# State-space steps on one Trainium2 core: the sums over states as quarter-array products

## What is computed

```python
delta = softplus(dt @ W_dt.T + b_dt)          # 512 channels
dA = exp(delta[..., None] * A)                # 16 states for each channel
dBx = delta[..., None] * Bm[:, :, None, :] * xc[..., None]
h = dA_t * h + dBx_t                          # scan over the 512 positions
y = einsum('bles,bls->ble', hs, Cm) + xc * Dp # sum over the 16 states, and the skip
y = y * silu(z)
out = einsum('ble,de->bld', y, W_out)
```

## Time and profile before

| what | value |
|---|---|
| median of 3 runs | 824.77 us (823.97 to 1462.39) |
| the profiled execution, its own time | 824.44 us |
| its span in the profile | 822.6 us |
| mean granted TensorE clock | 0.969 |

### The profile page before, as it was taken

One profiled execution on the slowest core, in us unless ns is written; L12 is line 12 of the kernel. 1 busy time (PEld: TensorE's weight loads), 2 busy tenths in 40 slices (PEclk: granted clock), 3 DMA queues, 4 the chain that ended last, 5 costly groups with the idle time before them and its releaser, 6 DMA issues.

```text
span 822.6 us, 10341 instructions
## 1 busy us (share of the span) xinstructions
PE 737.9 (90%) x3787; PEld 523.0 (64%) x3823; DVE 548.4 (67%) x962; ACT 395.8 (48%) x575; POOL 240.8 (29%) x182
## 2 busy tenths in 40 slices
PE   3899999996788899999999998996889998788997
PEld 3587565652435466667877886884547787435786
DVE  4444589999969999964456556358754655943543
ACT  3354596666465687732232343351375532274321
POOL 0000058775438587850896000001000000000000
PEclk9899999999999899999999998999799999999999
DMA  8300022222102222217001000033000142000000
GB/s 278 129 2 0 1 66 78 76 71 67 55 28 64 65 76 62 82 39 225 13 1 22 0 1 1 14 102 103 16 2 1 56 115 62 2 28 1 1 1 25
DMA packets 30591, 41.75 MB, mean 51 GB/s; under 512 B 3753, under 2 KB 19955, under 8 KB 30515
## 3 DMA queue, kind: packets, MB, share of 16 engines
q1 hardware_dynamic: 29290, 40.91, 16.7%
q10 hardware_dynamic: 1252, 0.19, 0.2%
HBM read 36.73 MB, written 4.26 MB: 50 GB/s over the span
## 4 chain that ended last, share of the span: by engine, by line
PE 64%; DVE 15%; issue 11%; ACT 4%; DMA 4%; SPq 2%; DVEq 0%
PE PS L489 34%; PE PS L859 7%; DVE PS L1947 4%; PE PS L589 3%; PE PS L1050 3%; PE PS L1067 3%; DVE shared L1955 2%; PE PS L634 2%; ACT shared L1543 2%; PE PS L843 1%; DVE route L2000 1%; PE PS L447 1%; DMA scratch_k<-shared 1%; DMA shared<-in_L_ffn_W_dram 1%; SPq L2212 1%
## 5 line engine op out<-in xcount | busy, mean ns | idle before, releaser
L2258 POOL TENSOR_TENSOR shared<-shared,route 128x1024 f32<-128x1024 f32 x64 | 151.4, 2368 | 78.7 <-DVE shared L1955 73.5
L489 PE MATMUL PS<-xnT,weights_r 128*128 128x256 f32 (+1 forms) x732 | 156.3, 361 | 0.5 <-issue 0.3
L489 PE MATMUL PS<-xnT,work_r 128*128 128x512 f32 (+1 forms) x596 | 150.4, 401 | 0.2 <-DVE gated L1723 0.2
L1955 DVE TENSOR_TENSOR_SCAN shared<-shared,PS 128x512 f32<-128x512 f32 x128 | 148.7, 1203 | 1.4 <-ACT shared L1487 1.4
L489 PEld LDWEIGHTS PS<-xnT,weights_r 128*128 128x128 f32 x732 | 115.4, 190 | 34.0 <-issue 20.1
L489 PEld LDWEIGHTS PS<-xnT,work_r 128*128 128x128 f32 (+1 forms) x596 | 110.7, 191 | 24.7 <-DVE gated L1723 0.4
L859 PE MATMUL PS<-shared,cf 128*128 128x512 f32 x256 | 124.7, 610 | 0.0
L1487 ACT ACTIVATE shared<-shared,cols 128x512 f32<-128x512 f32 x128 | 85.0, 715 | 29.6 <-DVE shared L1955 29.2
L1723 DVE TENSOR_TENSOR gated<-gated,PS 128x512 f32<-128x512 f32 (+1 forms) x52 | 35.6, 685 | 91.2 <-ACT gated L1235 91.1
L489 PE MATMUL PS<-weights_r,work_r 128*128 128x256 f32 (+1 forms) x624 | 92.5, 298 | 3.6 <-DVE work_r L1730 2.6
L489 PEld LDWEIGHTS PS<-weights_r,work_r 128*128 128x128 f32 (+1 forms) x624 | 82.1, 193 | 6.4 <-DVE work_r L1730 3.2
(11 more groups left out here) (218 smaller groups left out, 1027.2 us busy)
## 6 DMA issues: line engine op xcount, KB each, us to landing
route<-scratch_c SPq DMA_DIRECT2D x64, 256.0 KB, 3.2
shared<-in_L_ffn_W_dram SPq DMA_DIRECT2D x3, 1024.0 KB, 9.2
scratch_k<-shared SPq DMA_DIRECT2D x12, 128.0 KB
scratch_q<-shared SPq DMA_DIRECT2D x12, 128.0 KB
shared<-scratch_k SPq DMA_DIRECT2D x8, 192.0 KB
shared<-scratch_q SPq DMA_DIRECT2D x8, 192.0 KB
mamba_w<-in_L_ffn_w_dram SPq DMA_DIRECT2D x2, 704.0 KB, 5.5
beside<-in_L_ffn_w_dram SPq DMA_DIRECT2D x2, 704.0 KB, 7.6
```

The lines of the kernel that those rows point to most:

```text
L489: last = nc.tensor.matmul(o, lhs[l], rhs[r], start=(start and i == 0), stop=(stop and i == 2))
L1955: v.tensor_tensor_scan(hst[:, (t % 2 * 2 + j) * T:(t % 2 * 2 + j + 1) * T], decay[t % D_SLOTS][:, j * T:(j + 1) * T], products[:, j * T:(j ...
L2258: nc.gpsimd.tensor_tensor(hc[:, u * 2 * T:(u + 1) * 2 * T].rearrange("p (c t) -> p c t", c=2), hst[:, (t % 2) * 2 * T:(t % 2 + 1) * 2 * T] ...
```

## The change

`add_state` forms each of its two sums in two products of 64 rows by 64 columns, on four different quarters of the array. Rows 0 to 63 of chunk 0 go to partitions 0 to 63 of bank 4, rows 0 to 63 of chunk 1 to partitions 64 to 127 of bank 5; rows 64 to 127 of chunk 0 to partitions 64 to 127 of bank 4, and those of chunk 1 to partitions 0 to 63 of bank 5. So the two halves of chunk 1's sum lie crosswise in bank 5, and `add_skip` reads them with two instructions of 64 partitions in place of one of 128.

```diff
@@ -51,6 +51,7 @@
 SUM_BANKS = (4, 5)
+HALF_ROWS = (slice(0, 64), slice(64, 128))
@@ -855,10 +856,12 @@
                 def add_state(t, of=b):
                     pe.wait_ge(s["hc"], HEAD + of * STEPS + t + 1)
-                    for j in range(2):
-                        last = nc.tensor.matmul(bank(SUM_BANKS[j]), ident[:, :],
-                                                hc[:, (t % H_SLOTS * 2 + j) * T:(t % H_SLOTS * 2 + j + 1) * T],
-                                                start=False, stop=(t % DS == DS - 1))
+                    for r in HALF_ROWS:
+                        for j in range(2):
+                            o = HALF_ROWS[r.start // 64 ^ j]
+                            last = nc.tensor.matmul(bank(SUM_BANKS[j])[o, :], ident[r, r],
+                                                    hc[r, (t % H_SLOTS * 2 + j) * T:(t % H_SLOTS * 2 + j + 1) * T],
+                                                    start=False, stop=(t % DS == DS - 1))
                     last.then_inc(s["ys"], 1)
@@ -1914,10 +1917,13 @@
                 def add_skip(half, of=b):
 
                     dve.wait_ge(s["ys"], HEAD + of * STEPS + (half + 1) * DS)
-                    for j in range(2):
-                        x_ = xc_of[of][2 * half + j]
-                        v.scalar_tensor_tensor(x_, x_, c_D[:, 2 * half + j:2 * half + j + 1],
-                                               bank(SUM_BANKS[j]), ALU.mult, ALU.add).then_inc(s["yr"], 1)
+                    x_, d = xc_of[of][2 * half], c_D[:, 2 * half:2 * half + 1]
+                    v.scalar_tensor_tensor(x_, x_, d, bank(SUM_BANKS[0]), ALU.mult, ALU.add).then_inc(s["yr"], 1)
+                    for i, r in enumerate(HALF_ROWS):
+                        x_, d = xc_of[of][2 * half + 1][r, :], c_D[r, 2 * half + 1:2 * half + 2]
+                        last = v.scalar_tensor_tensor(x_, x_, d, bank(SUM_BANKS[1])[HALF_ROWS[1 - i], :],
+                                                      ALU.mult, ALU.add)
+                    last.then_inc(s["yr"], 1)
```

## The result

The changed kernel's median is 819.11 us (13 runs, 816.02 to 825.54), beside 823.97 us for the kernel before in the same rounds. One run of the kernel before fell out at 1462.39 us; all ratios here are of fast runs, without it. The ratio is 0.9944 with a 95% interval of 0.9924 to 0.9965, so 4.6 us less (2.9 to 6.3), clear of zero and far inside 2%. The forecast was 819.3 us, 5.5 less. The profiled execution has a span of 818.1 us against 822.6.

What follows compares the result with a forecast made beforehand. TensorE and VectorE both stood at about 3.4 us a step, so only waits, turn and end counted. -2.22 (last scan) - 2.0 (lag) - 1.24 (two calls) = -5.5 us gave 819.3 us, range 815 to 827.

Steps and rivals of the forecast that it cites:

- The frame: State-space steps: VectorE stays full at 3.42 us, so TensorE's savings count only where VectorE waits or TensorE carries the end.
- Two bunches of four, 1.0 to 1.2 us to the next product: Sign in `add_state`: eight records per call in two bunches, 1.0 to 1.2 us from it to the next product.
- Rivals 2, 3 and 4: `add_state`: row groups in turn (about 835 us, 0.06), passes strictly in order (about 856, 0.03), nothing side by side (930, 0.03).
- a saving of 0.62 us a call: Each `add_state` call on TensorE: 1.10 us, taken from the attention's nearest row, in place of 1.72.
- +0.66: `add_skip` on VectorE: one more instruction of 64 partitions costs 0.66 to 0.7 us, at three skips that count.
- The first skip: Batch 0, at 168.64: the wait of 0.38 us goes, an instruction of 0.66 comes, so +0.28.
- the turn: Between the batches: two `add_state` calls save 1.24 us, so VectorE's 4.66 us wait ends 1.24 sooner.
- "-2.22" for the last scan: Running sum after the skip at 311.24: VectorE ends its last scans 2.22 us earlier, at about 358.9.
- The lag at the end, "-2.0": After the last scan: TensorE, which opened the output 2.1 us late, keeps up and waits for the scan: -2.0 us.
- -1.24: After the last scan: two more `add_state` calls on the path, together 1.24 us less.
- "from the last scan to the residual 1.2 us less": Sign behind the steps: the stretch from the last scan to the residual gets 1.2 us shorter.
- Rival 1: TensorE idles more, so its clock falls twice more where it leads, turn and end: 824.7 us, no change; chance 0.14.

Runs made afterwards that it cites:

- e1: The change with quarter products and the three-instruction skip only in half 1 of each batch, full-width products and two-instruction skip in half 0; ratio to the kernel before 0.9944.
- e2: The change with chunk 1 not crosswise, so both chunks use the same two quarters, and the two-instruction skip; 831.1 us, ratio to the kernel before 1.0087.
- e6: The changed kernel, unchanged, for a second profile; 261.7 us from the first scan to the third `mamba_output`, against 263.2 in its first profile.
- e9: The changed kernel, unchanged, for a third profile; ratio to the kernel before 0.9942, 261.8 us from the first scan to the third `mamba_output`.
- e7: The change plus products of zeros that keep TensorE busy where it would wait for VectorE; ratio to the kernel before 0.9943.
- e5: The kernel before, unchanged, for a second profile; 267.9 us from the first scan to the third `mamba_output`, against 265.6 in its first.
- e11: The change with its four products in another order, both row halves of chunk 0 first, then both of chunk 1; ratio to the kernel before 0.9952.
- e4: The change with the two-instruction skip reading bank 5 straight, the halves of chunk 1's sum not put back in order; 814.33 us, ratio to the kernel before 0.9885.
- e3: The kernel before, full-width products kept, with chunk 1's skip in two instructions of 64 partitions; ratio to the kernel before 1.0020.
- e8: Quarter products and the three-instruction skip in half 1 only, plus zero products in TensorE's waits; ratio to the kernel before 0.9925.
- e10: Quarter products and three-instruction skip in half 1 only, plus zero products in TensorE's waits, timed again beside the change; ratio to the kernel before 0.9951.

## Why the prediction was right, and where its terms were not

- **The frame held.** VectorE's step stayed at 3.42 us, and 21.5 us less of TensorE's busy time (737.9 to 716.4) came to 4.6 of the time. e1 points the same way: half the calls, all the gain.
- **Two bunches of four, 1.0 to 1.2 us to the next product**: 1.02, bunches 0.48 us apart. Rivals 2, 3 and 4 fall; e2 gave the price of products that must queue.
- **"a saving of 0.62 us a call" was too large: 0.49.** Ahead of the group, the broadcast takes 0.32 us from start to start instead of 0.22, the 0.10 that the forecast had. Behind the group, the side work takes 0.11 longer: twelve side products up to the next broadcast take 1.53 (e2, 130.81 to 132.34) instead of 1.42, a float32 group up to the next full-width product 1.83 (365.61 to 367.44) instead of 1.72. Where the next product is again a group of quarters, the 0.10 ahead of it comes on top: 1.62 for the twelve (356.65 to 358.27), 1.93 for the float32 group (362.66 to 364.59). The likely reason for the 0.11 is the weight load of the first full-width product. Before, it ran under the last pass of `add_state`; after a group of quarters it starts only with its product (128.77), as the weight loads' timelines show, of before and then of the change:

```profile
129.41 0.19 PEld L489 LDWEIGHTS PS<-xnT,weights_r 128*128 128x128 f32 x1 [0.24 <-issue]
```

```profile
127.75 0.21 PEld L862 LDWEIGHTS PS<-shared,cf 64*64 64x64 f32 x8 [0.23 <-issue]
128.77 1.02 PEld L490 LDWEIGHTS PS<-xnT,weights_r 128*128 128x128 f32 x8 [0.81 <-issue]
```

  A call thus costs 0.10 + 1.02 + 0.11 = 1.23 us. The attention's rows, from which the 1.10 was taken, were read only up to the start of the next product, so what comes behind that start was left out. Two calls on the open path bear the 0.49 out: 1.0 us at the turn (e6) and 1.0 at the end.
- **"+0.66" for the third skip instruction was too small: 0.97 up to the next operation.** From start to start the pair of before takes 1.32, so 0.66 each; of the three, the first takes 0.75 (167.71 to 168.46) and the two halves 0.77 each (168.46 to 170.00). So the two that were there got longer as well. And the two products behind them take 1.33 up to the scan (170.00 to 171.33) instead of 1.19 (169.96 to 171.15 in before):

```profile
171.15 2.33 DVE L1955 TENSOR_TENSOR_SCAN shared<-shared,PS 128x512 f32<-128x512 f32 x2
```

  That makes 1.1 us at the first skips of the batches and 1.0 at the turn, where the scan comes right behind the skip. Why they start less closely behind one another wasn't tried.
- **The first skip** came out at +0.63 instead of +0.28 (its scan at 171.33 against 171.15, less the 0.45 of the head start), **the turn** shortened VectorE's wait from 4.66 to 3.94 us, 0.7 instead of 1.24; in e6, where the clock stayed up, to 3.65, 1.0.
- **"-2.22" for the last scan** was +0.25 in the first profile and -1.2 to -1.3 in e6 and e9. But 0.7 to 0.8 of the latter is the small instruction ahead of step 22, which the change doesn't touch; like for like it is -0.5. This is the step that was off most, by 1.7: three dearer skips make 1.2 of it, the smaller saving at the turn 0.2, and the rest are short new waits for a broadcast.
- **The lag at the end, "-2.0"**: from 2.1 to 0.4 us, so -1.7. From the opening to the third `mamba_output` it is 7.83 us (361.33 to 369.16) instead of 8.83, so -1.0 where -1.24 was forecast. The sign that the prediction named, "from the last scan to the residual 1.2 us less", left out its own lag of 2.0; it is 2.7 less (from 361.1 to 374.83 before, from 360.9 to 371.95 after).
- **Rival 1, the clock, was partly true.** Its "ahead of the turn the clock stood at 1.00" was a misreading: rows 12 are of the turn itself, and over 216 to 224 the kernel before had 0.79. In the first profile of the change the low level lay there (0.50). The change does lower the mean clock (e7's numbers above), but e5 shows the low level in the kernel before too, once at a worse place, and e7, with the clock back up, is no faster (what the added products themselves cost wasn't separated from that). So a spread of some 2 us by where the low clock falls is in the kernel before already, and no price of the change by the clock could be measured.

The total agreed better than its terms, and in part by luck. Like for like, the profiles have -0.5 - 1.7 - 1.0 = -3.2 us (3.9 against e5) where the sum had -5.5; the timed -4.6 has an interval 3.4 wide. What makes the time's middle larger than the steps' 3.2 stays open.

## What to carry to other kernels

Where two engines share a step and stand at nearly the same time, add up only the waits that the other engine has for yours, the turns between loops, and the tail; a saving elsewhere turns into idle time. The quarters paid here only with all four in flight (1.02 us a call, 1.87 on two, 1.72 full-width), and each group cost a change-over of about 0.1 us on both sides. A lag of the other engine need not show in the next step; it can come due at the next place where yours waits for its sum. A layout that comes out crosswise has a bill at the reader, and if the reader is the full engine it eats the gain: count its instructions by the time from one start to the next, the first operation behind them included.

## What the runs showed of the hardware that was not expected

- Eight passes of 64 x 64 float32 products, 512 columns each, on four quarters take 1.02 us with both row halves of one bank at work at once (the change, e11), on two quarters 1.87 (e2).
- The granted clock's low level moves from one execution to the next of the same kernel: over 216 to 224 and 224 to 232 it was 0.79 and 1.00 in the first profile of the kernel before, 1.00 and 0.79 in the second, and the steps were 2.3 us longer in the latter. The part behind the steps, the same in all kernels, took 445.1 to 453.4 us.
- A VectorE instruction on four elements for each partition, 0.17 us after the last step (e4, at 371.74), took 1.19 to 1.21 us ahead of step 22 in eight profiles (before, e5, the change, e1, e3, e4, e8, e10) and 0.38 to 0.83 in e2, e6, e9 and e11; in e7 its successor took 1.31. No run was made to find why.
